# A fused decoder layer: the second bank of transposed probabilities copied by ScalarE, and the last expert chunk's loads and products in another order

## The reference

```
def rmsnorm(x, gamma): return x / max(norm(x), 1e-12) * sqrt(128) * (gamma + 1)

# part 1: x (64, 128, 128)
y = pointwise(causal_depthwise_conv3(rmsnorm(x, g_conv))) + x
hidden, gate = split(rmsnorm(y, g_gru) @ w_hg.T)
h_t = (1 - sigmoid(gate)) * h_(t-1) + sigmoid(gate) * g(hidden)      # written in logs in the reference
y = h + y
y = gelu(rmsnorm(y, g_ff) @ w1.T + b1) @ w2.T + b2 + y
x = layernorm(x + y)

# part 2: cross attention, 16 heads of 64, context (64, 120, 128), causal mask
q, k, v = x @ Wq + bq, ctx @ Wk + bk, ctx @ Wv + bv
attn = softmax(q @ k.T / 8 + mask)
x = layernorm(x + (attn @ v) @ Wo + bo)

# part 3: mixture of 16 experts, the best 2 of each row, and a shared expert
p = sigmoid(x @ gate_w + gate_b); values, experts = top_k(p, 2); values /= sum(values)
out_e = (silu(x @ wg_e) * (x @ wu_e)) @ wd_e
x = layernorm(x + (x + shared(x) + sum of values * out_e of the two experts))
```

## Time and profile before

| what | value |
|---|---|
| median of 3 runs | 1649.22 us (1649.03 to 1649.48) |
| the profiled execution | 1656.81 us |
| its span in the profile | 1654.5 us |
| mean granted TensorE clock | 0.928 |
| TensorE busy | 1354.1 us, 82% |
| VectorE busy | 1097.8 us, 66% |
| ScalarE busy | 805.7 us, 49% |
| GpSimd busy | 837.0 us, 51% |

### The profile page before, as it was taken

How to read it: one execution, slowest core, us unless ns; L and a number is a source line. 1 busy time by engine, 2 the same in 40 slices (tenths; PEclk the granted TensorE clock), 3 DMA queues, 4 the chain that set the end, 5 groups by cost and what they waited for, 6 DMA issues and landing times. The chain is left out here.

```text
span 1654.5 us, 34065 instructions
## 1 busy us (share of the span) xinstructions
PE 1354.1 (82%) x11168; PEld 1098.7 (66%) x11168; DVE 1097.8 (66%) x2851; ACT 805.7 (49%) x3111; POOL 837.0 (51%) x996
## 2 busy tenths in 40 slices
PE   2879797889888888988888897988888898887650
PEld 1667575768676677767667775867767776765540
DVE  3566667676756777667776768666776767766233
ACT  3645554555546455554545554454645455452120
POOL 5342434543446536554556545664566545564344
PEclk9989999999999998999999999999999999999575
DMA  6000000032112212132122211132122222133551
GB/s 202 8 7 8 8 7 15 17 98 58 37 53 79 69 53 62 45 105 72 36 59 80 81 53 57 43 87 86 31 65 69 83 68 62 30 92 100 153 164 54
DMA packets 142895, 105.77 MB, mean 64 GB/s; under 512 B 12352, under 2 KB 137856, under 8 KB 142720
## 3 DMA queue, kind: packets, MB, share of 16 engines
q1 hardware_dynamic: 132224, 84.71, 17.7%
q0 software_dynamic: 8192, 16.79, 3.5%
q10 hardware_dynamic: 2304, 2.10, 0.4%
HBM read 69.99 MB, written 33.55 MB: 63 GB/s over the span
## 5 line engine op out<-in xcount | busy, mean ns | idle before, releaser
L1574 POOL TENSOR_TENSOR pr<-pr,ri 128x480 f32<-128x480 f32 x256 | 251.1, 991 | 324.8 <-DVE ri L1212 323.4
L904 ACT ACTIVATE pr<-sE,nm 128x120 f32<-128x120 f32 x512 | 178.0, 360 | 413.0 <-DVE nm L1197 412.8
L584 PE MATMUL pvb<-pT,vv 120*64 120x128 f32 x2048 | 147.0, 288 | 80.7 <-DVE pT L1208 79.9
L584 PEld LDWEIGHTS pvb<-pT,vv 120*64 120x64 f32 x2048 | 115.4, 142 | 112.3 <-DVE pT L1208 104.2
L904 ACT ACTIVATE pr<-sO,nm 128x120 f32<-128x120 f32 x512 | 179.4, 383 | 0.0
L552 PEld LDWEIGHTS sE<-kT,qT 64*128 64x128 f32 x1024 | 132.3, 199 | 57.4 <-issue 57.4
L1208 DVE COPY pT<-t 120x512 f32<-120x512 f32 x256 | 165.3, 684 | 7.6 <-PE t L411 6.5
L1614 POOL DMA_INDIRECT gat<-sorted_y,slot x128 | 128.3, 1002 | 63.1 <-issue 47.0
L552 PE MATMUL sE<-kT,qT 64*128 64x120 f32 x1024 | 156.4, 296 | 0.0
L552 PE MATMUL sO<-kT,qT 64*128 64x120 f32 x1024 | 156.4, 296 | 0.0
L411 PE MATMUL t<-ident_f,pr 128*120 128x128 f32 x1024 | 152.0, 297 | 3.7 <-POOL pr L1574 3.3
(11 more groups left out here) (332 smaller groups left out, 3453.2 us busy)
## 6 DMA issues: line engine op xcount, KB each, us to landing
wq<-in_w_e SPq DMA_DIRECT2D x224, 128.0 KB
sorted_y<-yq SPq DMA_DIRECT2D x64, 256.0 KB, 2.5
xq<-sorted_x SPq DMA_DIRECT2D x56, 256.0 KB, 2.8
xt<-in_x SPq DMA_DIRECT2D x16, 256.0 KB, 3.0
sorted_x<-yq SPq DMA_DIRECT2D x16, 256.0 KB, 4.0
out_y<-y SPq DMA_DIRECT2D x64, 64.0 KB, 1.6
cT<-in_ctxT SPq DMA_DIRECT2D x16, 240.0 KB, 3.0
sorted_x<-x,slot POOLq DMA_INDIRECT x128, 2.3
```

The source lines that it names most:

```text
L584: ins = mm(pvb[r * DK:(r + 1) * DK, (k // 2) * T:(k // 2 + 1) * T], vv[:, q, h * DK:(h + 1) * DK], pT[:, 4 * r + k // 2, :], start=True, s ...
L904: ins = f(pr[:, p % RING, r, i, :], score_banks[r][:, i * S:(i + 1) * S], ACT.Exp, bias=nm[:, p % 2, r, i:i + 1], accum_out=rsum[:, p % 2, ...
L1574: GP.tensor_tensor(pr[:, p % RING, r, :, :], pr[:, p % RING, r, :, :], ri[:, p % 2, r, :, :].to_broadcast([P, 4, S]), ALU.mult).then_inc(s ...
```

## The change

`b_probs_T` used to have VectorE copy both banks of transposed probabilities. Now VectorE copies `t0` and ScalarE copies `t1`, at the start of step `s`, before the exponentials of that step. The semaphore `probsT_sb` becomes two, `probsT0_sb` and `probsT1_sb`, and TensorE waits for the one, the other or both. In the last chunk SyncE loads the rows of quads 56 to 63 ahead of the store of quad 54 and, of the weights, now loads quads 58 to 61 behind it; ScalarE loads 56, 57, 62 and 63 (before: SyncE 56 to 59, ScalarE 60 to 63). After the loop VectorE does the products of quads 56 to 59 ahead of any sum, and those of later quads behind two sums. SyncE stores quads in another order against the results.

```diff
@@ -68,7 +68,7 @@
     "ctx_hi": 1, "ctx_split": 1, "proj": 24, "proj_act": 12, "proj_dve": 12, "scores": 16, "negmax": 16, "probs": 16,
-    "probsT": 16, "probsT_sb": 16, "rinv": 16, "normal": 16, "pv": 8, "headsT_sb": 8,
+    "probsT": 16, "probsT0_sb": 8, "probsT1_sb": 8, "rinv": 16, "normal": 16, "pv": 8, "headsT_sb": 8,
     "wo": 4, "attn_sum": 4, "ln2_stats": 4, "ln2_mv": 4, "ln2_eps": 4, "ln2_rstd": 4, "ln2_out": 4,
@@ -313,7 +313,7 @@
                 k = n // quads
-                if n % quads == 0:
+                if n % quads == 0 or last(n):
                     sp.wait_ge(sem["expert"], upto("expert", k))
@@ -370,12 +370,12 @@
                     sp.wait_ge(sem["a_bank"], whole("a_bank", G - 1))
-                    for i in range(2):
-                        w_load(LAST + i)
-                        d_store(QUADS * d + 2 + i)
                     for i in range(quads):
                         x_load(LAST + i)
-                    for i in range(2, 4):
+                    d_store(QUADS * d + 2)
+                    w_load(LAST + 2)
+                    d_store(QUADS * d + 3)
+                    for i in (3, 4, 5):
                         w_load(LAST + i)
@@ -390,8 +390,13 @@
             pipeline(body)
-            for i in range(quads):
+            for i in range(6):
                 d_store(LAST + i)
+            for i in range(2):
+                e_store(G - 4, i)
+            for i in range(6, quads):
+                d_store(LAST + i)
+            for i in range(2, 2 * SEQ):
                 e_store(G - 4 + i // SEQ, i % SEQ)
@@ -507,7 +512,7 @@
                     if later(b):
-                        pe.wait_ge(sem["probsT_sb"], upto("probsT_sb", b - 1, 14 + n - 4))
+                        pe.wait_ge(sem[f"probsT{n - 4}_sb"], whole(f"probsT{n - 4}_sb", b - 1))
                 else:
@@ -558,7 +563,7 @@
                     if p:
-                        pe.wait_ge(sem["probsT_sb"], upto("probsT_sb", b, 2 * p - 2 + r))
+                        pe.wait_ge(sem[f"probsT{r}_sb"], upto(f"probsT{r}_sb", b, p - 1))
                     elif r == 0:
@@ -571,7 +576,8 @@
                 q, half = p // 2, p % 2
-                pe.wait_ge(sem["probsT_sb"], upto("probsT_sb", b, 2 * p + 1))
+                for r in range(2):
+                    pe.wait_ge(sem[f"probsT{r}_sb"], upto(f"probsT{r}_sb", b, p))
                 if half:
@@ -661,7 +667,7 @@
                 if n == LAST + 1:
-                    pe.wait_ge(sem["probsT_sb"], whole("probsT_sb", G - 1))
+                    pe.wait_ge(sem["probsT1_sb"], whole("probsT1_sb", G - 1))
                 elif n % QUADS or c is None:
@@ -891,6 +897,14 @@
+            def b_probs_T(b, p):
+                if p:
+                    act.wait_ge(sem["pv"], upto("pv", b, p - 1))
+                elif later(b):
+                    act.wait_ge(sem["pv"], whole("pv", b - 1))
+                act.wait_ge(sem["probsT"], upto("probsT", b, 2 * p + 1))
+                f(pT[:, 4:8, :], seqs(t1[0:S, :]), ACT.Copy).then_inc(sem["probsT1_sb"], 1)
+
             def b_probs(b, p, r):
@@ -998,6 +1012,8 @@
                 for s in range(PAIRS + LAG):
+                    if B and s >= LAG:
+                        b_probs_T(b, s - LAG)
                     if B and 0 < s < PAIRS:
@@ -1013,7 +1029,7 @@
                     if c == G - 1 and s > 1 and s % 2 == 0:
-                        w_load(LAST + 4 + s // 2 - 1)
+                        w_load(LAST + (0, 1, 6, 7)[s // 2 - 1])
                     if A:
@@ -1203,9 +1219,8 @@
                         dve.wait_ge(sem["pv"], whole("pv", b - 1))
-                for k in range(2):
-                    dve.wait_ge(sem["probsT"], upto("probsT", b, 2 * p + k))
-                    V.tensor_copy(pT[:, 4 * k:4 * k + 4, :], seqs((t0, t1)[k][0:S, :])).then_inc(sem["probsT_sb"], 1)
+                dve.wait_ge(sem["probsT"], upto("probsT", b, 2 * p))
+                V.tensor_copy(pT[:, 0:4, :], seqs(t0[0:S, :])).then_inc(sem["probsT0_sb"], 1)
@@ -1469,14 +1484,18 @@
             pipeline(body)
+            for i in range(4):
+                d_act(LAST + i)
             for i in range(0, quads + 2, 2):
...
                     if j < quads:
+                        e_sum(G - 4 + j // SEQ, j % SEQ)
+                for j in range(i + 4, i + 6):
+                    if j < quads:
                         d_act(LAST + j)
-                        e_sum(G - 4 + j // SEQ, j % SEQ)
             for i in range(0, 2 * SEQ + 2, 2):
...
                     if j >= 0:
```

## The result

The changed kernel takes 1597.85 us (median of four runs, 1595.77 to 1600.01) against 1649.12 us (1648.31 to 1649.48), a ratio of 0.9688 with a 95% interval of 0.9675 to 0.9701: 51 us less. Forecast were 1587 us in a range of 1563 to 1618. The profiled execution took 1600.01 us.

A forecast was written before the change was run, and what follows sets the result against it. The prediction took a cycle of waits between VectorE and ScalarE in the pair steps as the bound. Copy 41.4, clock 15 and last chunk 6 make 62.4 us off 1649.2: 1587 us, range 1563 to 1618.

The forecast's parts named there:

- Part 1: Pair steps: one copy fewer on VectorE saves 0.6 us in each of 69 steps whose maximum VectorE delays: 41.4 us.
- The cover on ScalarE: Pair steps: ScalarE's copy of 0.6 us fits into its wait for maxima, 1.46 us at the tightest, and costs nothing.
- (c): Middle steps: TensorE's own work becomes the bound, half of the 41.4 us arrives, no clock gain: 1622 us, chance 0.12.
- (d): Pair steps: ScalarE's copy delays the exponentials, up to 0.6 us in 128 steps: at worst 1679 us, chance 0.04.
- (e): Pair steps: something other than VectorE bounds them, copies only turn into waiting: 1643 to 1649 us, chance 0.04.
- Part 2: Step 7: TensorE's clock drop after idle gaps is avoided in some six of 14 groups, up to 2.35 us each: 15 us.
- the first gap: Step 6: TensorE's idle time before the values product, waiting for both copies, forecast to shrink from 2.25 to about 1.05 us.
- Part 3: Last chunk: earlier row loads and weights divided anew let the last two groups' gathers start at 1613, not 1619.07: 6 us.
- the second gap: Step 6: TensorE's idle time waiting for VectorE's recurrence, forecast to stay at 1.42 us.
- (a): Whole kernel: copies and last chunk give what is counted, the clock still drops in each group: 1602 us, chance 0.26.
- (b): Whole kernel: the clock stays up in all 14 groups: 1569 us, chance 0.12.
- the ring: Pair steps: cycle of waits from maxima to exponentials, reciprocals, VectorE's other work, the copies and the next maxima.

The follow-up runs named there:

- copied_twice: The changed kernel with VectorE copying bank t0 twice into the same place, a wait between: 1720.67 us, ratio 1.0071 to the kernel before.
- scalar_twice: The changed kernel with ScalarE copying bank t1 twice into the same place, a wait between: 1596.89 us, ratio 0.9681 to the kernel before.
- before_filled: The kernel before, with small matmuls in both of TensorE's idle gaps of step 6 (nine and six): 1633.14 us against 1647.89, ratio 0.9912.
- second_gap_filled: The changed kernel with six small matmuls before the recurrence's transposition only: 1585.71 us, ratio 0.9627 to the kernel before.
- chunk_alone: The kernel before with only the last chunk's edits, both copies still on VectorE: 1705.21 us against 1707.6, ratio 0.9991.
- all_together: The changed kernel with both gaps filled, VectorE's group 12 sums earlier and weights of quads 58 and 59 issued earlier: 1576.38 us against 1647.89, ratio 0.9562.

## Why the prediction was right, and where it was not

**Part 1, right.** 41.4 us were forecast for 69 late maxima. Over all 16 groups, the distances from the maximum of step 0 to that of step 6 add up to 764.5 us before and 719.5 after the change: 45.0 less. A few single steps gave more than a copy (one of the first group fell from 9.11 to 6.59 us). In the later groups the saving can be read off as well: from one maximum to the next it was 10.03, 6.35, 8.37, 6.95 and 10.37 us in the group at 791.9, and 9.42, 5.74, 7.85, 6.36 and 9.58 in the group at 766.8 after the change, 3.12 us in five steps, 0.62 each. `copied_twice` took it back. The scores did not become the bound (54 waits, 59 before). The cover on ScalarE held: in step 3, where the earlier trace rows had 2.06 us, 0.97 are left behind the copy (1.46 less the copy of 0.61, so 0.85, were forecast), and `scalar_twice` added a copy to it without a loss. ScalarE's row in that step now:

```profile
790.41 0.36 ACT L918 ACTIVATE pr<-sE,nm 128x120 f32<-128x120 f32 x1 [0.97 <-DVE nm L1213]
```

Rivals (c), (d) and (e) fall.

**Part 2, near in size, wrong in the way.** 15 us were forecast. From the maximum of step 6 to that of step 7 the 16 groups took 124.7 us before and 113.2 after: 11.4 less, which with the 45.0 above and 0.8 lost elsewhere is the 55.7 us of the result. By the granted clock, time at 1.2 GHz fell from 238 us (2 x 0.072 x 1654.5) to 169 (2 x 0.053 x 1598.3). Of the 11.4 us, 9.4 come from the five groups in which the clock now holds, 1.9 each where 2.35 was the unit. The other 2.1 come from the ten in which it still falls, in some of them later than before; for these the prediction had put nothing. That such an amount is there to be had is shown by `before_filled`: 14.8 us with the clock up in all 15 groups.

The way was wrong. The prediction put its hope in the first gap, which "shrinks from 2.25 us to about 1.05". It did shrink, to 1.2 or 1.7 us in the later groups, and yet the groups with 1.23 us fall and most with 1.7 hold. Not even the idle time of both gaps together sorts them: one falls with 1.82 us, another holds with 3.19. That five groups hold where six were guessed is therefore luck. `second_gap_filled` shows that filling the second gap, which the change doesn't touch, keeps the clock up in 13 of 15. The term also counted 14 groups; a step 7 of this kind is in 15.

Forecast (a), the clock falling in every group, would have been 1602 us and (b) 1569; the kernel lies between, 4 us from (a), because part 3 gave nothing. The Trainium skill's page "TensorE: Matmul & The Clock Gate", section "A second HAM failure mode: psum-queue depth-cycling", says that frequent short idle times between groups of matmuls make the clock swing. The traces agree: in the kernel before all 15 groups fall, and with both gaps filled none does. That such gaps have to go and not merely shrink was my own inference from it, and this change, with five groups won, speaks against the zero that I drew from it.

**Part 3, the step that failed.** "That is 6 us" was about 0: `chunk_alone` gives 1.5 us and at most some 4, from the last scatter to the end the two profiled executions have 92.0 and 92.25 us, and the gathers of group 14 stand at +56.8 where the forecast had +50.5. Two terms were off. The first gather comes at +18.2 rather than +16.8, and the chain to group 14 takes 38.6 us (1562.88 - 1524.24) rather than 30.7 + 3. "With VectorE's products of quads 59 to 63 between the sums I add 3 us" left out that VectorE's queue is in order: the products of quads 58 and 59 wait for weights that SyncE issues only behind the rows and two stores, and the first sum waits behind them. I had priced SyncE's weight loads for TensorE and not followed the wait to VectorE. The prediction named the sign: gathers of group 12 more than 4 us later, and they were 4.4. By the Trainium skill's page "DMA: Bandwidth & Descriptors", section "Issuing engines are not separate DMA queues", dividing loads over engines saves issue time only. The last chunk's edits together gave about 0, which doesn't speak against it; the division of weights was not run by itself. In `all_together` the same bytes are issued 17 to 29 us earlier against the last scatter by the same engine, and are part of the 6 to 8 us gained there.

**The sum.** 62.4 us were forecast and 51 measured. The profiled spans differ by 56.2 us: parts 1 and 2 came out to within a microsecond, and six are missing, all of part 3. The other five are in how the profiled executions stand to their medians: before, 7.7 us above, after, 2.2, and the forecast had taken the same distance off both. So the near match of 56.4 and 55.7 us is in part luck: an ordinary execution of the kernel before is shorter than the one profiled, and by the medians the copy and the clock gave 51.

**Open.** Why the clock falls in some groups and not in others: the ten that fall have first gaps of 0.40 to 2.17 us, the five that hold 0.65 to 1.74, with a second of 1.4 in nearly all. Whether filling the first gap alone would do as well. Why `copied_twice` is 3 us slower beyond its wait.

## What to carry to other kernels

Find the ring and count its late steps: here work moved off the engine that closes the ring paid its full length in each of them, and an engine that waits inside the ring took it for nothing. Where transfers are moved forward in a queue, follow each of the later ones to the first instruction that waits for it, and then down the in-order queue of that engine. Idle time of TensorE can be worth filling with work whose result nobody reads; here filling the gap right ahead of the fall paid in most groups, while shortening the earlier one paid in a third of them, and not in the one where it became shortest (0.40 us).

## What was not expected of the hardware

**Slower chips.** The kernel before takes 3.5% more on chip 14 (1707.6 against 1649.1 us) and nearly as much on chip 10. In the changed kernel's trace from chip 10, the step from the maximum of `sE` in step 0 to that in step 1 takes 14.0 to 15.5 us in six groups, 9.9 in one and mostly 7.7 in the others; on the first chip it is 7.7 in all but the first group. VectorE waits there for TensorE, and TensorE stands still for nothing that the profile shows. VectorE first, then TensorE:

```profile
1073.54 0.69 DVE L1203 COPY vv<-t 120x512 f32<-120x512 f32 x1 [8.17 <-remote]
```
```profile
1070.02 0.47 PE L420 MATMUL t<-wv_s_hi,cS_hi 128*120 128x512 f32 x1 [1.64 <-issue]
1072.14 0.59 PE L421 MATMUL t<-wv_s_lo,cS_hi 128*120 128x512 f32 x1 [1.65 <-issue]
```

The cause isn't known. The groups in which the clock falls are others there, and fewer: the filling of two gaps is worth some 6 us on chip 14 and the filling of one some 11 on chip 8. That the longer steps shift the falls isn't shown.

**Filling pays by itself.** Fifteen matmuls of 0.2 us a group that compute nothing take 14.8 us off the kernel before (ratio 0.9912, 0.9896 to 0.9929).
